# Attention and mixture-of-experts kernel: two ternary matrices, the output weight and the router are prepared later, and SyncE issues every raw load

## The reference

```
k = concatenate([x1 @ Wk1, x2 @ Wk2]);  v = concatenate([x1 @ Wv1, x2 @ Wv2])
x = x + softmax(q k^T * scale) v @ Wo + bo
```

```
scale = clip(mean(abs(W), axis=-1), 1e-5)
w_q   = clip(round(W / scale), -1, 1) * scale
h     = layernorm(x) * gamma + beta
x     = x + silu(h @ sw1.T) @ sw2.T + gate * (silu(h @ ew1[e].T) @ ew2[e].T)
```

## Time and profile before

| | |
|---|---|
| median of 3 runs | 833.96 us (831.59 to 834.95) |
| the profiled execution | 833.6 us, of which the span in the trace is 831.8 us |
| busy over the span | PE 83%, PEld 59%, DVE 76%, ACT 79%, POOL 76% |
| the last weighing of values for unit 255 ends | about 644 us |
| the routed experts | about 700 to 830 us |

### The profile page before, as it was taken

How to read it: one execution, slowest core, us unless ns; L and a number is a source line. 1 busy time by engine, 2 the same in 40 slices (tenths; PEclk the granted TensorE clock), 3 DMA queues, 4 the chain that set the end, 5 groups by cost and what they waited for, 6 DMA issues and landing times.

```text
span 831.8 us, 21620 instructions
## 1 busy us (share of the span) xinstructions
PE 686.6 (83%) x7878; PEld 488.0 (59%) x7878; DVE 631.6 (76%) x1188; ACT 654.6 (79%) x1430; POOL 634.6 (76%) x673
## 2 busy tenths in 40 slices
PE   4559898999999998999989998999986425888883
PEld 3226566676667666576766666676754313766662
DVE  3657787787878787787869787787863387899994
ACT  4357899989899998899889989989997202788882
POOL 1055788989799998989888988889898543577773
PEclk9678999999999999999999999999999857899998
DMA  7148989798989789898989799797889002344410
GB/s 240 39 89 165 175 145 186 150 186 160 190 148 193 170 155 186 138 192 175 176 159 182 156 161 191 143 187 153 171 149 178 26 2 71 99 126 129 133 60 8
DMA packets 325337, 119.41 MB, mean 144 GB/s; under 512 B 293475, under 2 KB 318573, under 8 KB 325234
## 3 DMA queue, kind: packets, MB, share of 16 engines
q1 hardware_dynamic: 319954, 104.39, 65.3%
q0 software_dynamic: 5280, 13.64, 5.6%
HBM read 35.40 MB, written 13.50 MB: 59 GB/s over the span
## 4 chain that ended last, share of the span: by engine, by line
POOL 27%; DVE 21%; PE 15%; ACT 14%; DMA 12%; issue 9%; SPq 1%; DVEq 1%; ACTq 0%; POOLq 0%
POOL p_split L506 12%; DMA pt<-p_split 10%; PE FB L311 4%; ACT probs L749 4%; POOL above L502 4%; POOL row L544 3%; DVE x L1106 3%; ACT p_split L683 3%; DVE w_raw L1120 2%; DVE pt L1116 2%; POOL gate L524 2%; POOL ht_lo L548 2%; DVE neg_max L1045 2%; DVE o_sb L1112 2%; PE S L1223 2%
## 5 line engine op out<-in xcount | busy, mean ns | idle before, releaser
L506 POOL TENSOR_TENSOR p_split<-probs,p_split 128x512 f16<-128x512 f32 x256 | 310.0, 1218 | 65.3 <-ACT p_split L683 63.4
L749 ACT ACTIVATE probs<-S,neg_max 128x512 f32<-128x512 f32 x256 | 175.2, 684 | 24.8 <-DVE neg_max L1045 21.2
L683 ACT ACTIVATE p_split<-probs 128x512 f16<-128x512 f32 x256 | 160.8, 628 | 13.7 <-DMA pt<-p_split 7.3
L1045 DVE TENSOR_REDUCE neg_max<-S 128x1 f32<-128x512 f32 x256 | 170.5, 678 | 0.1
L311 PE MATMUL FB<-xt_hi,w_split 128*128 128x256 f16 x768 | 144.5, 280 | 8.9 <-DVE xt_lo L875 6.2
L1239 PE MATMUL O<-v_st,pt 128*128 128x64 f16 x1024 | 116.7, 195 | 21.4 <-DMA pt<-p_split 20.6
L1239 PEld LDWEIGHTS O<-v_st,pt 128*128 128x128 f16 x1024 | 92.7, 98 | 64.3 <-DMA pt<-p_split 34.9
L1240 PE MATMUL O<-v_st,pt 128*128 128x64 f16 x1024 | 115.7, 194 | 0.0
L1241 PE MATMUL O<-v_st,pt 128*128 128x64 f16 x1024 | 115.7, 194 | 0.0
L1223 PE MATMUL S<-k_st,q_st 64*128 64x512 f16 x768 | 107.1, 385 | 7.9 <-ACT probs L749 7.9
L311 PE MATMUL FB<-xt_lo,w_split 128*128 128x256 f16 x384 | 107.3, 279 | 0.0
(11 more groups left out here) (223 smaller groups left out, 1875.1 us busy)
## 6 DMA issues: line engine op xcount, KB each, us to landing
rows<-row SPq DMA_DIRECT2D x32, 256.0 KB, 2.6
w_raw<-in_L_ffn_expert_w SPq DMA_DIRECT2D x15, 512.0 KB, 4.5
c_in<-in_ctx SPq DMA_DIRECT2D x16, 256.0 KB, 3.2
x_in<-in_x SPq DMA_DIRECT2D x16, 256.0 KB, 3.1
xb<-in_x SPq DMA_DIRECT2D x16, 256.0 KB, 3.2
pt<-p_split SPq DMA_TRANSPOSE x256, 3.3
k_st<-in_L_xattn_Wk SPq DMA_DIRECT2D x2, 512.0 KB, 6.8
w_split<-rows,p_split POOLq DMA_INDIRECT x39, 3.5
```

The costliest lines, as they stand in the source:

```text
L506: g.tensor_tensor(p_split[n % HL_RING][:, 1, :], probs[n % PROBS_RING][:, :], p_split[n % HL_RING][:, 0, :], ALU.subtract).then_inc(p_lo_r ...
L683: a_(p_split[g % HL_RING][:, 0, :], probs[g % PROBS_RING][:, :], ACT.Copy).then_inc(p_hi_ready, 1)
L749: a_(probs[n % PROBS_RING][:, :], S[n % 4][:, :], ACT.Exp, bias=neg_max[:, n % 4:n % 4 + 1], accum_out=sums[:, n % UNITS:n % UNITS + 1]).t ...
L1045: v.tensor_reduce(neg_max[:, n % 4:n % 4 + 1], S[n % 4][:, :], AX.X, ALU.max, negate=True)\
```

## The change

Nothing that is computed changes. What moves:

- A table `EXTRA_AT` gives three matrices beside the regular ones: number 0 is now the shared **down** matrix, at n = 0; number 2 the shared **up** matrix, at n = 18; number 17, the last, the **up** matrix of expert 0, at n = 243. Each is loaded by SP at 2 units ahead of that n, DVE sums and POOL scales at n, DVE compares at n + 1 and n + 2, POOL takes the difference at n + 3, and SP turns it at n + 4. The down matrix of expert 0 becomes number 1, and the others f + 1.
- `row_sums` on ACT, `row_scale` and the difference on DVE, and the two loads by POOL are gone.
- `WEIGHTS_AT`: Wq, Wk1 and Wk2 go from -15, -14, -13 to -13, -12, -11, Wv2 and Wv1 to -7 and -6, and Wo from -6 to 3. `PREP_AT`: router and bias go from -6 and -5 to 4 and 5.
- At the start SP no longer loads a raw matrix, and loads Wo behind the small ones. The wait for `half_up_ready` goes to the first tanh, and the first use of the shared up matrix waits for three turned matrices in place of one.

```diff
-WEIGHTS_AT = {-15: 0, -14: 1, -13: 2, -8: 3, -7: 4, -6: 5}
+EXTRA_AT = {0: (0, E, True), 18: (2, E, False), 243: (2 * E + 1, 0, False)}
+EXTRA_LOAD, EXTRA_SUM, EXTRA_SCALE, EXTRA_ABOVE, EXTRA_UNDER, EXTRA_TERN, EXTRA_TURN = -2, 0, 0, 1, 2, 3, 4
+WEIGHTS_AT = {-13: 0, -12: 1, -11: 2, -7: 3, -6: 4, 3: 5}
...
-PREP_AT = {-6: ROUTER_W, -5: BIAS, 7: SHARED_ROW}
+PREP_AT = {4: ROUTER_W, 5: BIAS, 7: SHARED_ROW}
...
+        def matrix_of(f):
+
+            return {1: 1}.get(f, f + 1)
+
+        def extra(n, at):
+
+            return EXTRA_AT.get(n - at)
...
-            def load_raw(f):
-                sp.wait_ge(tern_ready, f + 2)
-                e, down = f // 2, f % 2 == 1
-                sp.dma_start(raw_down if down else raw_up, (ew2_v if down else ew1_v)[e]).then_inc(raw_loaded, 16)
+            def load_raw(m, e, down):
+                at_least(sp, tern_ready, m)
+                if e == E:
+                    src = (sw2 if down else sw1).rearrange("(c p) f -> p c f", p=P)
+                else:
+                    src = (ew2_v if down else ew1_v)[e]
+                sp.dma_start(raw_down if down else raw_up, src).then_inc(raw_loaded, 16)
...
-                if n == -6:
-                    pool.wait_ge(tern_ready, 1)
-                    g.dma_start(out=raw_up, in_=ew1_v[0]).then_inc(raw_by_pool, 16)
-                if n == -1:
-                    ternary(1)
-                    pool.wait_ge(tern_ready, 2)
-                    g.dma_start(out=raw_down, in_=sw2.rearrange("(c p) f -> p c f", p=P)).then_inc(raw_by_pool, 16)
+                if extra(n, EXTRA_TERN):
+                    ternary(extra(n, EXTRA_TERN)[0])
...
-                if n == -9:
-                    row_sums(0, False)
-                if n == -5:
-                    row_sums(1, False)
-                if n == 1:
-                    row_sums(2, True)
...
-                    if n < 3:
-                        row_scale(n, e, cols, width, raw, down)
-                    else:
-                        dve.wait_ge(raw_loaded, (n - 1) * 16)
-                        dve.wait_ge(half_ready, n * 3)
-                        v.tensor_reduce(w_abs[:, 0:cols], raw, AX.X, ALU.add, apply_absolute_value=True)\
-                            .then_inc(abs_ready, 1)
+                    dve.wait_ge(raw_loaded, (n + 1) * 16)
+                    at_least(dve, half_ready, n * 3)
+                    v.tensor_reduce(w_abs[:, 0:cols], raw, AX.X, ALU.add, apply_absolute_value=True)\
+                        .then_inc(abs_ready, 1)
...
-                dve.wait_ge(sign_ready, n * 2 + 2)
-                v.tensor_tensor(above[:, :], above[:, :], under[:, :], ALU.subtract).then_inc(tern_ready, 1)
...
-                for stage in {-8: (0,), -7: (1,), -6: (2, 3)}.get(n, ()):
-                    quantise(0, E, False, stage)
-                for stage in {-4: (0,), -3: (1,), -2: (2,)}.get(n, ()):
-                    quantise(1, 0, False, stage)
-                for stage in {2: (0,), 3: (1,), 4: (2, 3)}.get(n, ()):
-                    quantise(2, E, True, stage)
+                for stage, at in enumerate((EXTRA_SUM, EXTRA_ABOVE, EXTRA_UNDER)):
+                    if extra(n, at):
+                        quantise(*extra(n, at), stage)
```

More of the change, by code:

```diff
@@ L436, in _ @@
                 if f is not None and f > 0:
-                    load_raw(f)
+                    load_raw(matrix_of(f), f // 2, f % 2 == 1)
+                if extra(n, EXTRA_LOAD):
+                    load_raw(*extra(n, EXTRA_LOAD))
                 t = due(n, STORE_H)
@@ L451, in _ @@
                     turn_probs(n - 1)
-                if n == -5:
[L453 to L457, removed]
+                if extra(n, EXTRA_TURN):
+                    turn_ternary(*extra(n, EXTRA_TURN))
                 f = due(n, TURN_W)
                 if f is not None and f > 0:
-                    turn_ternary(f + 2, f // 2, f % 2 == 1)
+                    turn_ternary(matrix_of(f), f // 2, f % 2 == 1)
         @block.gpsimd
@@ L516, in row_scale @@
                 g.tensor_scalar(w_half[:, 1, 0:cols], w_abs[:, 0:cols], -0.5, None, ALU.mult).then_inc(half_ready, 1)
+                if e == E and not down:
+                    g.tensor_scalar(half_up[:, :], w_abs[:, :], 0.5, None, ALU.mult).then_inc(half_up_ready, 1)
                 dst = (down_scale if down else up_scale)[:, e, 0:cols]
@@ L576, in _ @@
                 if f is not None and f > 0:
[L577 removed]
+                    row_scale(matrix_of(f), f // 2, f % 2 == 1)
+                if extra(n, EXTRA_SCALE):
+                    row_scale(*extra(n, EXTRA_SCALE))
                 f = due(n, TERN_W)
                 if f is not None and f > 0:
[L580 to L587 removed]
+                    ternary(matrix_of(f))
+                if extra(n, EXTRA_TERN):
+                    ternary(extra(n, EXTRA_TERN)[0])
                 if n == LAST_T + HT_LO + 1:
@@ L711, in tanh_up @@
                 act.wait_ge(up_full, t * 2 + j + 1)
+                if t == 0:
+                    act.wait_ge(half_up_ready, 1)
                 for c in range(2):
@@ L840, in quantise @@
                     return
-                dve.wait_ge(sign_ready, n * 2 + 2)
-                v.tensor_tensor(above[:, :], above[:, :], under[:, :], ALU.subtract).then_inc(tern_ready, 1)
-            def row_scale(n, e, cols, width, raw, down):
-                dve.wait_ge(abs_ready, n + 1)
-                v.tensor_scalar(w_abs[:, 0:cols], w_abs[:, 0:cols], 1.0 / width, EPS, ALU.mult, ALU.max)\
-                    .then_inc(scale_ready, 1)
-                dve.wait_ge(scale_ready, n + 1)
-                v.tensor_scalar(w_half[:, 0, 0:cols], w_abs[:, 0:cols], 0.5, None, ALU.mult).then_inc(half_ready, 1)
-                v.tensor_scalar(w_half[:, 1, 0:cols], w_abs[:, 0:cols], -0.5, None, ALU.mult).then_inc(half_ready, 1)
-                dst = (down_scale if down else up_scale)[:, bass.ds(e, 1), 0:cols].rearrange("p a c -> p (a c)")
-                v.tensor_scalar(dst, w_abs[:, 0:cols], 1.0 / HSCALE if down else HSCALE / 2, None, ALU.mult)\
-                    .then_inc(half_ready, 1)
-                if is_static(n) and n == 0:
-                    v.tensor_scalar(half_up[:, :], w_abs[:, :], 0.5, None, ALU.mult).then_inc(half_up_ready, 1)
             def settle(s, value):
@@ L1088, in _ @@
                     if f is not None and f > 0:
-                        quantise(f + 2, f // 2, f % 2 == 1, stage)
+                        quantise(matrix_of(f), f // 2, f % 2 == 1, stage)
                 for j in range(FRONT):
@@ L1296, in up_shared @@
                     if t == 0:
-                        pe.wait_ge(tern_moved, 16)
+                        pe.wait_ge(tern_moved, 48)
                 else:
```

13 lines of the change are left out of this document (4 added, 9 removed).

## The result

The changed kernel takes 828.9 us in the median of 14 runs (823.8 to 834.8), the kernel before 834.3 (828.7 to 836.2); the ratio is 0.993 (0.991 to 0.995). It is faster, by 5.4 us where 12 were forecast. The ratios in this document leave out runs more than 1.5% above the fastest of their kernel, which leaves two of combo_2's six. The profiled execution has a span of 827.4 us.

What follows compares the result with a forecast made beforehand. No single engine was the bound; the start was taken as a serial chain of raw loads, sums, comparisons and difference, with little room after it. 833.6 - 20.5 + 3.5 + 5.0 = 821.6, given as 822 us, range 812 to 829.

Steps and rivals of the forecast that it cites:

- Unit 18, 3.5 (0 to 7): Units 18 to 32: the added shared up matrix costs 3.5 us, between 0 and 7.
- ScalarE has 3.8 us idle of 36, so at best nearly all is recovered: Lower bound at unit 18: ScalarE's idle time could absorb the added matrix, a cost of 0.
- 1 to 2 us: Sign to look for: VectorE's wait for the raw matrix before the row sums of unit 18.
- The version of the sum by the Trainium skill: Unit 18: both comparisons meet GpSimd at the shared ports, 0.9 us more each, so 5.3 instead of 3.5.
- Unit 243, 5 (1.5 to 9): Near the end of the units: the last matrix's late load, sums and GpSimd work cost 5 us, between 1.5 and 9.
- The start, 20.5: Sequence 0 up to unit 7: three matrices, Wo, router and bias leave the front, gaining 20.5 us (19.3 to 21.9).
- the walk: Step-by-step timing of the new start: first exponential near 30.3 us, exponentials 1 to 5 from 32.3 to 42.2.
- Wo at 3: Start: converting Wo at unit 3, with half a weight at 1.2 us on VectorE.
- Q0 at 44.9, clock in the middle: Sequence 1: Q0 starts near 44.9 us instead of 64.31; unit 7 midway between low clock (50.8) and high (48.2).
- What follows the last exponential takes the same: Tail behind the units: its time should not change.
- the two late loads cost all they can: Rival, 16%: at units 18 and 243 every engine waits in line, costing 7 and 9 us; time 829.
- The shift never heals: Rival, 4%: from unit 18 both comparisons meet GpSimd in every later sequence, 23 us over 13 sequences; time 845.

Runs made afterwards that it cites:

- combo_2: The change with the matrix of unit 18 loaded at 15 and spread, the last matrix loaded at 257, behind all turned probabilities; ratio 0.973 to the kernel before.
- no_late: The change without the matrices at units 18 and 243, constants in their place; ratio 0.975 to the kernel before.
- early_load: The change with its two late loads issued one unit earlier (15 and 240 instead of 16 and 241); ratio 0.994 to the kernel before.
- spread_243: The change with the last matrix spread among the units: load 240, sums 243, comparisons 246 and 248, difference 250; ratio 0.997 to the kernel before.

## Why the prediction was off

The mechanisms were named, but the prices of the new places were too low and the gain at the start too high. The first three points are these terms, in the order of their error.

- *Unit 18, 3.5 (0 to 7)*: 6.9 in that execution, 5.4 to 7.6 in seven. This is the step that failed most: "ScalarE has 3.8 us idle of 36, so at best nearly all is recovered", from which 3.5 was taken. Nothing was recovered. The load itself came as forecast: issued at 71.17 and there at 75.70, the forecast 89.9 and 94.5 less 18.6 to within 0.2. VectorE reached the sums at 72.40 (91.0 less 18.6) and waited 3.30 us. The prediction's own times say 3.5; its "1 to 2 us" under the signs is what that exceeds the idle time of before. By unit 19 the wait had cost 1.8 (2.4 by early_load over the whole stretch). But VectorE, not ScalarE, is full at units 19 and 20, so both comparisons cost their whole 1.9 and 2.0 us: 5.6 at unit 21. Nothing of it was made up by unit 32: 6.9 are lost there, and 1.3 are lost in no_late without the matrix. The version of the sum by the Trainium skill (page SBUF — State Buffer, section "Who interferes with whom"; 5.3) was nearer: both comparisons ran beside a GpSimd instruction, at 1.94 and 2.02 us. With the load a unit earlier and the steps spread, the loss is 2.5 to 3.9.
- *Unit 243, 5 (1.5 to 9)*: 6.1 to 7.1 in five kernels. The wait was shorter than forecast (1.47 for 1.9 to 3.6) and unit 244 2.6 late for a forecast 3.1 to 4.8; the line behind it was longer. 1.1 to 1.4 us are the load, 1.7 GpSimd's difference; these may overlap. That the rest is GpSimd's queue fits with spread_243, where 3.4 us less were lost up to the last exponential and 2.1 came back behind it, but isn't taken apart further.
- *The start, 20.5*: 18.6 in that execution, 18.3 in the mean of eleven. The first exponential was right to 0.6 us (30.94 for 30.3), the walk to unit 4 not (43.00 for 40.6). The step that failed here is "Wo at 3" at 1.2 us: it took 2.93, beside GpSimd's difference, which the walk had placed at the same unit. With Wo at unit 6 the start gave 19.2 to 21.0. The rule of the Trainium skill that I weighed at the comparisons of unit 18 (same page and section) belonged here as well, at a larger instruction.
- *Q0 at 44.9, clock in the middle*: TensorE waited 3.69 us for the router's low half, until 44.77, and that was late behind Wo. The bias and the weighings followed in 2.4, as forecast, so Q0 started at 47.19. Unit 7 came 4.6 behind Q0, just the middle that I took between the two clock levels (0.78 over 48 to 52 us), 18.4 earlier and not 20.5. From unit 7 to 15 nothing moved, as said.
- *"What follows the last exponential takes the same"*: true of the work. 1.9 us more went with a lower clock in this execution and 0.5 in the next. The forecast had put this at nothing.
- *Sum*: 833.6 - 18.6 + 6.9 - 1.8 + 7.1 + 1.9 = 829.1, the 829.2 of the profiled execution. The time is that of the rival "the two late loads cost all they can", to which I gave 16%. It named the mechanism, though the line behind the loads carries more of it than the loads. That its 829 fits to the microsecond is luck: its gain at the start (20.5) and its loss at unit 243 (9) were both 1.9 too large and cancel, and a drift of 1.8 that nobody forecast or explained made up for the clock. "The shift never heals" fell: sequences 2 to 14 kept their length within the drift.

## What to carry to other kernels

Work taken off a serial start isn't won until it has a place: here 18.6 us were gained and 14 paid back at two places. The idle time that counts is that of the engine that gets the work, in those very units: VectorE had none at units 19 and 20, whatever ScalarE had over 36 us. Here a load of 512 KB wanted three units of lead and not two, and the comparisons cost less two units apart (3.1 us on average at unit 18, 4.1 with the earlier load alone). Where GpSimd was full as well, spreading only pushed work on; a stretch in which the engines wait anyway took it. The same three matrices and Wo, placed so, gave 16 us instead of 5. When an instruction of VectorE with two inputs moves, look up what GpSimd does in the same unit.

## What was not expected

The clock behind the last exponential differs between executions of one program (0.73 and 1.00 over 8 us, 0.51 in another kernel), and the end moves with it by some 2 to 3.5 us; what decides it stays open. So does the drift of up to 2.2 us between units 32 and 243. And converting Wo ahead of unit 0 let unit 7 start as early, yet cost 4 to 5 us at unit 12: the later start had only pushed the next raw load behind its sums.
